# A projection chunk between transposition and attended product in every fourth slot of a fused cross-attention and mixture-of-experts kernel

## What is computed

```python
q = rms_norm(linear(x, q_w, q_b), norm_q_w).reshape(B, L, NH, HD)
k = rms_norm(linear(ctx_txt, k_w, k_b), norm_k_w).reshape(B, -1, NH, HD)
v = linear(ctx_txt, v_w, v_b).reshape(B, -1, NH, HD)
k_img = rms_norm(linear(ctx_img, k_img_w, k_img_b), norm_k_img_w).reshape(B, -1, NH, HD)
v_img = linear(ctx_img, v_img_w, v_img_b).reshape(B, -1, NH, HD)
out = (attention(q, k, v) + attention(q, k_img, v_img)).reshape(B, L, DIM)
x = x + linear(out, o_w, o_b)          # the input of q is the layer norm of x
# then, on the layer norm of the new x:
h = gelu(x @ W1 + b1); h = gelu(h @ W2 + b2); eo = h @ W3 + b3     # for each expert
x = x + sum over the top two experts of softmax(x @ Wg + bg) * eo
```

## Time and profile before

| | |
|---|---|
| median of three runs | 842.35 us (840.61 to 843.66) |
| the profiled execution | 840.39 us |
| its span | 838.5 us |
| TensorE matmul busy | 759.5 us, 91% of the span |
| VectorE busy | 599.0 us, 71% |
| ScalarE busy | 491.5 us, 59% |
| GpSimd busy | 240.5 us, 29% |
| chain that ended last | TensorE 70%, VectorE 11%, ScalarE 10%, issue 5% |

### The profile page before, as it was taken

The page is one execution under the profiler, slowest core; times in us unless marked ns, Lnnn a source line. Parts: engine busy times, 40 slices in busy tenths (PEclk is TensorE's granted clock), DMA queues, the critical chain, the costliest instruction groups (busy, mean ns, idle before and its releaser), DMA issues.

```text
span 838.5 us, 17282 instructions
## 1 busy us (share of the span) xinstructions
PE 759.5 (91%) x5906; PEld 658.8 (79%) x5906; DVE 599.0 (71%) x1269; ACT 491.5 (59%) x1136; POOL 240.5 (29%) x302
## 2 busy tenths in 40 slices
PE   4889899989898989775499999999999999999994
PEld 3657677767676767454499999999999999999993
DVE  6767878787878796765576868576676858676664
ACT  4377777777777767585154645555554555554443
POOL 3523334343434242214300504032140505032010
PEclk9989999999999999776599999999999999999998
DMA  9720102011111110232755665748575665748561
GB/s 315 281 81 6 58 4 68 27 51 44 35 61 35 60 32 17 87 121 84 258 194 189 246 223 222 247 154 291 212 249 198 245 230 217 253 163 288 197 218 64
DMA packets 29205, 126.28 MB, mean 151 GB/s; under 512 B 4204, under 2 KB 4220, under 8 KB 19424
## 3 DMA queue, kind: packets, MB, share of 16 engines
q1 hardware_dynamic: 23696, 109.80, 37.1%
q0 software_dynamic: 5456, 15.81, 5.3%
HBM read 108.42 MB, written 18.74 MB: 152 GB/s over the span
## 4 chain that ended last, share of the span: by engine, by line
PE 70%; DVE 11%; ACT 10%; issue 5%; DMA 2%; POOL 1%; SPq 0%; ACTq 0%; DVEq 0%; POOLq 0%
PE tiles L1174 7%; PE tiles L1176 6%; PE tiles L1175 6%; PE scores L1463 4%; PE scores L1461 4%; PE ptb L1289 4%; PE scores L1462 4%; PE pvb L1176 3%; PE pvb L1175 3%; PE ptb L1175 3%; PE pvb L1174 3%; PE ptb L1174 3%; PE ptb L1176 3%; PE scores L1279 2%; PE pvb L1312 2%
## 5 line engine op out<-in xcount | busy, mean ns | idle before, releaser
L918 DVE TENSOR_TENSOR w<-scr,w 128x2048 fp32r<-128x2048 f32 x75 | 170.8, 2289 | 59.4 <-ACT w L682 59.4
L682 ACT ACTIVATE w<-scr 128x2048 fp32r<-128x2048 f32 x76 | 144.8, 1908 | 54.9 <-PE scores L1463 54.9
L512 POOL DMA_INDIRECT out_dram<-scr,tok x17 | 18.0, 1059 | 301.7 <-DVE scr L1153 299.3
L664 ACT ACTIVATE scr<-scr,rsum 112x257 f32<-112x257 f32 x128 | 66.4, 519 | 61.7 <-DVE rsum L902 61.7
L1174 PE MATMUL tiles<-c,w 128*128 128x258 f32 (+2 forms) x272 | 80.4, 296 | 4.7 <-DVE c L1127 2.6
L1174 PE MATMUL tiles<-w 128*128 128x256 f32 (+1 forms) x288 | 82.9, 288 | 0.6
L1175 PE MATMUL tiles<-w 128*128 128x256 f32 (+1 forms) x288 | 81.2, 282 | 0.0
L1176 PE MATMUL tiles<-w 128*128 128x256 f32 (+1 forms) x288 | 81.2, 282 | 0.0
L1141 DVE CAST w<-scr 128x256 fp32r<-128x256 f32 (+1 forms) x144 | 42.0, 292 | 54.6 <-ACT scr L772 54.6
L1289 PE MATMUL ptb<-ident,scr 112*128 112x112 f32 x384 | 63.9, 277 | 18.0 <-ACT scr L672 16.4
L1175 PE MATMUL tiles<-c,w 128*128 128x258 f32 (+2 forms) x272 | 77.8, 286 | 0.0
(11 more groups left out here) (221 smaller groups left out, 2302.2 us busy)
## 6 DMA issues: line engine op xcount, KB each, us to landing
scr<-in_dram SPq DMA_DIRECT2D x76, 1024.0 KB, 4.9
scr<-in_dram SPq DMA_DIRECT2D x8, 750.0 KB, 5.1
scr<-slots_d SPq DMA_DIRECT2D x10, 528.0 KB, 5.4
scr<-in_dram SPq DMA_DIRECT2D x10, 512.0 KB, 8.2
slots_d<-rows SPq DMA_DIRECT2D x8, 528.0 KB, 11.6
xn<-in_dram SPq DMA_DIRECT2D x9, 256.0 KB
xb<-in_dram SPq DMA_DIRECT2D x8, 224.0 KB, 2.7
xr<-in_dram SPq DMA_DIRECT2D x8, 224.0 KB, 2.6
```

The costliest lines, as they stand in the source:

```text
L664: act.activation(probs[0:L, s, 0:IMG], probs[0:L, s, 0:IMG], ACT.Copy, scale=rsum[0:L, g, s, 0:1]).then_inc(S["normal_img"], 1)
L682: act.activation(EH[slot], raw[slot], ACT.Copy).then_inc(S["eh_done"], 1)
L918: dve.tensor_tensor(EL[slot], raw[slot], EH[slot].bitcast(F32), ALU.subtract).then_inc(S["el_done"], 1)
```

## The change

VectorE's `attended` moves to a later place in its slot: in slot 2 behind the routing choice, in slots 6, 10 and 14 behind everything else that the slot has. On TensorE, the BIG pieces of slots 2, 6, 10 and 14 move from the end of the slot to between the transposition and `attend`. Pieces of these slots are all in BIG, so nothing remains at their end. Nothing else is changed, and no instruction is added or removed.

```diff
--- before.py
+++ after.py
@@ -1023,8 +1023,6 @@
                     if h == 10 and has_prep(b):
                         add_squares(b, 0)
                         add_squares(b, 1)
-                    if h in (6, 10, 14) and has_heads(b):
-                        attended(b, (h - 6) // 4)
                     if h == 10 and has_prep(b):
                         add_sums(b)
                     if h in (7, 11, 15) and has_heads(b):
@@ -1032,8 +1030,6 @@
                     if h in KEYS_AT and (has_prep if h > 1 else has_heads)(b):
                         c, step = KEYS_AT[h]
                         normalise_keys(p if step else 1 - p, c)
-                    if h == 2 and has_tail(b):
-                        attended(b - 1, 3)
                     if h == 3 and has_tail(b):
                         attended_low(b - 1, 3)
                     if h == 1 and has_prep(b):
@@ -1072,6 +1068,10 @@
                         gate_weights(b - 2)
                     if h == (1 if fixed(b, DONE) else 2) and has_route(b):
                         gate_choice(b - 2)
+                    if h == 2 and has_tail(b):
+                        attended(b - 1, 3)
+                    if h in (6, 10, 14) and has_heads(b):
+                        attended(b, (h - 6) // 4)
                     if h == (7 if fixed(b, DONE) else 3) and has_route(b):
                         gate_slots(b - 2)
                     if h == 12 and fixed(b, DONE):
@@ -1330,6 +1330,8 @@
                             transpose(b - 1, NH - LAG + h)
                     elif has_heads(b):
                         transpose(b, h - LAG)
+                    if h % 4 == 2:
+                        big(b, p, h)
                     if h == 2 and has_tail(b):
                         attend(b - 1, 1 - p, 3)
                     if h in (6, 10, 14) and has_heads(b):
@@ -1359,12 +1361,18 @@
                     if fixed(b, DONE) and h == 0:
                         stage("o", 0, 3, b, p)
                     for name, lo, hi in FILL[h]:
-                        if has(name, b) and not (fixed(b, DONE) and hi < NC):
+                        if has(name, b) and not (fixed(b, DONE) and hi < NC) and not (h % 4 == 2 and name in BIG):
                             stage(name, lo, hi, b, p)
                     if h == 0 and fixed(b, FIRST):
                         pe.wait_ge(S["small_in"], 64)
                     if h == 15 and fixed(b, FIRST):
                         pe.wait_ge(S["ol_done"], NC)
+
+            def big(b, p, h):
+
+                for name, lo, hi in FILL[h]:
+                    if name in BIG and has(name, b) and not (fixed(b, DONE) and hi < NC):
+                        stage(name, lo, hi, b, p)
 
             def values_of_last_image_keys():
 
```

## The result

The changed kernel takes 855.81 us (median of six runs, 855.33 to 857.53), the kernel before 841.54 beside it. The ratio is 1.0173, 95% interval 1.0161 to 1.0186: about 14 us slower, where the forecast was no change and the range ended at 847.0. The profiled execution has a span of 853.4 us against 838.5.

The account below looks back on a forecast made before the run. Each batch was taken as a loop bound by TensorE in slots 3 to 13, then VectorE. Terms 0.4 + 1.2 + 2.5 - 1.7 - 2.3 = +0.1 us on 840.39 gave 840.5, as median 842.4; range 839.5 to 847.0.

Parts of the forecast that it names:

- The step that failed: Slots 14 and 15: TensorE is late by 0.65 to 1.3 us, which its gaps of slots 0 to 3 take up.
- a logits wait of over 1 us: Slot 15, a foretold trace reading: logits wait over 1 us instead of 0.44.
- The term beside it: Slots 14 and 15: VectorE reads the logits later, 0.35 us in batches 1 to 5; +2.5 in all, bounds 1.7 and 4.4.
- the cheap end: Slot 14: VectorE keeps the port against GpSimd's copy, so both key instructions are through in 0.67 us.
- Rival 1: Slots 14 and 2: contention goes against VectorE, port term 4.4, rank gain 0; +3.7 us, 846.1; chance 0.30.
- the sign that it named: Slot 14: the first key instruction takes more than some 0.7 us.
- Order on TensorE: Chunk ahead of attend, 28 places: +0.05 us in each of 7 slots 6, none in slots 10; +0.4, bounds -1.3 and +1.4.
- Squares product: Slot 10: TensorE's squares product waits for the later attended values, +0.17 us in 7 batches; +1.2, bounds 0.7 and 1.4.
- Rank: Slots 2 and 3: the routing comparison runs free ahead of attended, rank 0.43 us earlier in 4 batches; -1.7, other bound 0.
- The last batch: Slots 2 and 6: routing choice and residual work run in VectorE's waits for attend; -2.3 us, bounds -3.2 and -1.0.
- its upper bound of 1.4 us: TensorE's order: tiling mode changes drain, the new order behind a 512-wide chunk, which could cost up to +1.4 us.

Follow-up runs that it names:

- Run 5: Kernel before, with only VectorE's attended of slot 14 moved behind the key instructions; 853.55 us, ratio 1.0136.
- Run 4: The whole change plus six extra 512-column matmuls on TensorE in slot 15 of batches 0 to 6, where it would wait; 845.99 us, ratio 1.0052.
- run 3: The whole change, but with VectorE's attended of slot 14 put back in its old place; 844.84 us, ratio 1.0034.
- run 1: Kernel before with only VectorE's half of the change, TensorE's order as before; 854.17 us, ratio 1.015.
- run 8: Kernel before with attended late in slots 2 and 6, and slot 15's logits behind the chunk and read last by VectorE; 835.13 us, ratio 0.992.
- run 7: Kernel before with slot 15's logits behind the chunk on TensorE and read by VectorE at the slot's end; 838.42 us, ratio 0.9962.
- Run 6: Kernel before with VectorE's attended late in slots 2 and 6 only, chunks as before; 837.51 us, ratio 0.9938.
- run 2: Kernel before with only TensorE's half of the change, VectorE's attended early as before; 862.9 us, ratio 1.0249.

## Why the prediction was wrong

**The step that failed** is the sentence on slots 14 and 15: "TensorE is late by 0.65 to 1.3 in both cases, which its gaps of slots 0 to 3 take up." The place, the instruction and the contention with the copy were right. TensorE's lateness was 2.36 - 0.92 = 1.44 us, and a logits wait of over 1 us was even foretold. But an idle stretch was treated as time that can be made good later at the same speed. It could not: the clock fell behind it, the chunk and the scores ran at half speed, and VectorE, the bound of that part of the loop, came to wait for TensorE. The prediction put the clock at nothing without a reason, though the kernel before has a half-clock stretch at the same place in two batches. Run 5 shows that the late values of slot 14 alone cost 12 us. Run 4, whose only edit is the added work, shows the clock's part: with the same late values the clock stays full (mean over the whole kernel 0.96 in all five executions, against 0.94 in the change and 0.95 before) and the time falls by 10 us. In the four steady batches 5.36 of the 10.24 us lost are the clock.

**The term beside it was too small.** Slots 14 and 15 were put at 0.35 us a batch, bound 0.68. VectorE's reading of the logits came 3.32 us behind the transposition against 2.56, so 0.76 late. This is the other half of the loss: at full clock the steady batches of run 4 are 1.1 to 1.5 us longer than before, where the prediction's terms for such a batch add up to nearly nothing (0.05 + 0.17 + 0.35 - 0.43 = 0.14). Against run 3, which has the late values in the other slots only (43.28 and 43.65 at full clock), 0.5 to 0.9 of it belong to slots 14 and 15, the added work included. I chose the cheap end by the row in which VectorE won against GpSimd. In the changed kernel VectorE did win with the first key instruction (0.47) and lost with the second (1.12): the row was read rightly for one instruction and carried over to two. Rival 1 named this contention, and its sign was right; it came true in slot 14 only, while the comparison of slot 2 ran free, and not by the sign that it named: the first key instruction took 0.47, below its 0.7. Its 846.1 holds no term for the clock. That run 4, with the clock full, comes to 846.0 bears it out only roughly, since run 4 adds work and loses two half-clock stretches that the kernel before has. The fall of the clock was in no rival.

**What held.** Order on TensorE: +0.05 in slot 6, measured 0.07; the total effect of the order, given late values, is about the 2 us between run 1 and the change (1.015 against 1.0173), and their intervals overlap. Squares product: +0.17, measured 0.22. Rank: -0.43, measured 3.10 - 3.57 = -0.47, for the reason given; but that is its place in the slot. A whole batch gets less from it: with slots 2 and 6 late, run 8's steady batches are 0.17 us shorter than run 7's (171.70 against 172.37 us for four).

The last batch: -2.3. Its signs held in the change: rank comes 10.41 us behind the reading of the logits in place of 11.87, and VectorE's wait in slot 6 is gone. Run 6 shows -2.9 for the batch, but the change itself got only 0.5 (356.58 to 399.64, so 43.1 against 43.5). From the attended values of slot 14 to the last ones it takes 7.91 us in place of 6.97, of which 6.1 are at half clock in place of 4.3. That the clock took part of the gain back is likely, but was not tried.

**The pages named.** The Trainium skill, "TensorEngine Tiling (Array Packing)", "Key Properties", says that a change of tiling mode drains TensorE; the prediction took that as a reason for its upper bound of 1.4 us. The runs bear out no more than the 0.07 of slot 6, and slot 10 came 0.05 shorter. The Trainium skill, "GPSIMD Engine Reference", "Key points", says that GpSimd contends with VectorE instructions that have two SBUF inputs; the 1.12 agrees. The rule that mattered was not weighed: the Trainium skill, "TensorE: Matmul & The Clock Gate", "Part 1: The HAM clock gate (the "warmup" mystery)", says that the clock is set by how busy TensorE has recently been. The trace agrees where the wait is long: 1.74 us busy in 3.8, then PEclk 0.50. It leaves open the waits of 0.44 us, which were followed by a fall in some batches and not in others.

## What to carry to other kernels

In this kernel a wait of 1.9 us on TensorE was not paid back by later slack, because the clock fell behind it. Look up PEclk behind each place where TensorE goes idle, in the kernel before too, and price both the wait and the fall. Then price them apart: a run with work put into the wait shows what the clock costs, and what stays is the lateness, here about half. If a wait can't be taken away, put independent work ahead of it; here a chunk that was already in the slot, with the reader moved behind it as well, saved 16 us. And when an instruction moves behind others on one engine, ask which engine stands idle for its result, even if the queue itself loses nothing.

## What the runs showed of the hardware

Adding 42 matmuls of 512 columns made the kernel 10 us faster, because the granted clock stayed at 1.00 instead of 0.95 from 60 to 350 us. The half-clock stretches of the steady batches that were looked at lasted 3.4 or 6.8 us and stood right behind idle time of TensorE. But the same wait of 0.44 us at the logits was followed by one in batches 3, 4 and 6 of run 3 and by none in the three others, and in the kernel before by one in batches 1 and 6 and by none in the four others. What decides between these is open. And two halves of one change, 12 us (run 1) and 21 us (run 2) dear by themselves, cost 14 together.
